# Reordered last batch, mask as a bank term, weight parts turned by DMA, and 16-bit views in a six-layer kernel

## The reference

```python
x = x + cross_attention0(layernorm(x), ctx)   # 16 heads of 32, biases bq bk bv, out: concat @ Wo + bo
x = x + state_space(layernorm(x))
# block feed-forward: 16 blocks of 128, of which each token keeps the 4 most probable
prob = softmax(xf @ router_w.T + router_b); mask = top 4 of 16
h = relu(where(mask, x @ w1_block + b1_block, 0))
x = x + (where(mask, h, 0) @ w2 + b2)
x = x + cross_attention1(...); x = x + self_attention(...)
# quantised feed-forward, H = 512, I = 1536
up   = act_qdq(act_qdq(x) @ dequant(w_up).T)      # act_qdq: scale = max|.| / 32767, round, clip, * scale
gate = act_qdq(act_qdq(x) @ dequant(w_gate).T)
sig  = round(sigmoid(gate) * 65536) clipped to 65535, / 65536
gate = act_qdq(gate * sig); o = act_qdq(gate * up)
x = x + o @ dequant(w_down).T                     # dequant: blocks of 32 columns, 4 bits
```

## Time and profile before

| | us |
|---|---|
| median of 3 runs (lowest, highest) | 1790.96 (1788.42, 1792.11) |
| the profiled execution's own time | 1786.74 |
| span of its trace | 1785.0 |

### The profile page before, as it was taken

How to read it: one execution, slowest core, us unless ns; L and a number is a source line. 1 busy time by engine, 2 the same in 40 slices (tenths; PEclk the granted TensorE clock), 3 DMA queues, 4 the chain that set the end, 5 groups by cost and what they waited for, 6 DMA issues and landing times. The chain is left out here.

```text
span 1785.0 us, 34095 instructions
## 1 busy us (share of the span) xinstructions
PE 1586.5 (89%) x13897; PEld 828.1 (46%) x14008; DVE 1181.6 (66%) x1991; ACT 914.9 (51%) x1259; POOL 800.0 (45%) x406
## 2 busy tenths in 40 slices
PE   5999999999999999987689899899789989699359
PEld 2445555555555555543346464345434444344124
DVE  6688888888888888883455467779522233527881
ACT  1378888787877888773273133311112222228750
POOL 2277887888888888863108514522000000003310
PEclk9999999999999999998799979999899999899779
DMA  3589999999999999997316541234748944000001
GB/s 137 141 150 197 193 189 192 188 191 191 195 189 191 193 195 196 190 165 160 85 53 214 166 195 54 77 123 129 283 167 326 399 165 193 1 1 1 0 1 48
DMA packets 517543, 273.31 MB, mean 153 GB/s; under 512 B 443776, under 2 KB 495488, under 8 KB 514320
## 3 DMA queue, kind: packets, MB, share of 16 engines
q1 hardware_dynamic: 517392, 271.18, 63.3%
HBM read 138.74 MB, written 22.54 MB: 90 GB/s over the span
## 5 line engine op out<-in xcount | busy, mean ns | idle before, releaser
L553 POOL TENSOR_TENSOR x<-x_prob,x 128x1604 bf16<-128x1604 f32 x120 | 388.0, 3233 | 145.0 <-ACT x L708 145.0
L831 DVE TENSOR_REDUCE x_negmax<-x_score 128x1 f32<-128x1604 f32 x128 | 233.5, 1824 | 15.7 <-PE x_score L594 5.9
L690 ACT ACTIVATE x_prob<-x_score,x_negmax 128x1604 f32<-128x1604 f32 x128 | 204.8, 1600 | 43.9 <-DVE x_negmax L831 39.0
L577 PE MATMUL x_ring<-x_ctx_hi,wk_split 128*128 128x400 bf16 (+1 forms) x1024 | 216.2, 333 | 0.3 <-DVE x_kT L767 0.3
L577 PE MATMUL x_ring<-wv_split,x_ctx_hi 128*128 128x512 bf16 (+1 forms) x770 | 200.3, 379 | 9.7 <-issue 7.0
L767 DVE SCALAR_TENSOR_TENSOR x_kT<-x_ring,bk,x_kT 128x400 bf16<-128x400 f32 (+1 forms) x256 | 162.1, 634 | 31.9 <-ACT x_kT L679 23.9
L708 ACT CAST x<-x_prob 128x1604 bf16<-128x1604 f32 x120 | 183.0, 1525 | 0.0
L773 DVE TENSOR_TENSOR x_v<-x_ring,x_v 128x512 bf16<-128x512 f32 (+1 forms) x208 | 143.7, 691 | 52.9 <-ACT x_v L683 50.1
L679 ACT ACTIVATE x_kT<-x_ring,bk 128x400 bf16<-128x400 f32 (+1 forms) x196 | 116.0, 592 | 71.8 <-PE x_ring L577 71.0
L610 PE MATMUL x_pv<-x_pT,x_v 128*64 128x128 bf16 (+1 forms) x3328 | 119.9, 223 | 27.7 <-DVE x_kT L794 17.0
L683 ACT CAST x_v<-x_ring 128x512 bf16<-128x512 f32 (+1 forms) x148 | 86.5, 585 | 98.5 <-PE x_ring L577 98.3
(11 more groups left out here) (336 smaller groups left out, 2576.5 us busy)
## 6 DMA issues: line engine op xcount, KB each, us to landing
y_ctx<-in_ctx SPq DMA_DIRECT2D x16, 1664.0 KB, 10.6
y_ctxT<-in_ctxT SPq DMA_DIRECT2D x16, 1601.0 KB, 13.9
x_stage<-in_ctxT SPq DMA_DIRECT2D x48, 400.0 KB, 4.5
x_q_rows<-q_rows SPq DMA_DIRECT2D x64, 128.0 KB, 3.2
m_xT<-in_L_ffn_w SPq DMA_DIRECT2D x16, 512.0 KB, 4.8
ffn_w_parts<-m_xT SPq DMA_DIRECT2D x32, 256.0 KB, 2.6
x_stage<-in_ctxT SPq DMA_DIRECT2D x16, 401.0 KB, 5.0
f_w<-ffn_w_parts SPq DMA_DIRECT2D x4, 1024.0 KB, 9.8
```

The source lines that it names most:

```text
L553: pool.tensor_tensor(ph[:, g % 2, 1, 0:NKP], prob[:, g % 2, :], ph[:, g % 2, 0, 0:NKP], ALU.subtract).then_inc(pl_done, 1)
L577: last = pe.matmul(out_, lhs, rhs, start=(i == 0), stop=(i == len(steps) - 1))
L690: nc.scalar.activation(prob[:, g % 2, :].rearrange("p (c n) -> p c n", n=QW), scores, ACT.Exp, bias=nmax[:, g % 2:g % 2 + 1], accum_out=rs ...
L831: dve.tensor_reduce(nmax[:, pair % 2:pair % 2 + 1], scores, mybir.AxisListType.XY, ALU.max, negate=True).then_inc(max_done, 1)
```

## The change

Four parts.

1. Cross attention 0, last batch: the output tile comes directly behind the scores instead of last in the slot. bv no longer goes through `catT`; a product of bv with Wo in slot 0 ("bias") is added to bo, which now lies in `stage` and is loaded at g = LAST - 3. x is loaded again in eight DMAs spread over slots 2 to 6. DVE makes the last pair's low part instead of POOL. In slot 2 of that batch ACT finishes its pair before it copies the folded bank. At the kernel's start POOL splits the first context batch before it makes `picks`, `tri` and `low`.
2. Block feed-forward: the mask is turned into 0 or -1e30 and added by the mask product into the hidden bank itself, so that ACT's relu gives the masked value; six banks instead of three; DVE's multiply is gone. Four groups are computed before the first mask product.
3. `Dequant`: PE's transposes are replaced by two DMA transposes of the 16-bit parts on SP; ACT and DVE read the piece from SBUF; 17 pieces lie in the hidden layer and 19 in the second; a slot is loaded again when DVE's low part is done.
4. Quantised feed-forward: half of xhat is made by ACT. Rounded values stay in float32 with the large constant and are read as 16-bit integers with a step of two (`whole`, `fraction`), so the steps that remove the constant go away; all elementwise products are DVE's; maxima over partitions go over a PE transpose and a DVE reduction from bank 0. The gate chain ends one tile earlier, and its peak (n = 2) is turned by PE ahead of the last up group. Behind the up products ACT rounds gate for the first three tiles, then up and gate in turn. The last split begins with half a tile.

```diff
 # batch_plan
+        if b == B - 1:
+            steps.append(("tile", p - 1) if p else ("bias", 0))
         if 2 <= NPAIR * b + p < NPAIR * B + 2:
             steps.append(("pv", NPAIR * b + p - 2))
         if b and p == 2:
             steps.append(("out", b - 1))
-        if b == B - 1 and p:
-            steps.append(("tile", p - 1))
 # cross0_batches, SP
+        X_BEHIND = {2: (0,), 3: (1, 2), 4: (3,), 5: (4, 5), 6: (6, 7)}
+                    for t in X_BEHIND.get(g - LAST, ()):
+                        sp.dma_start(home_x[:, t, :], xv[:, t, :]).then_inc(x_in, 16)
 # PE
+            def bias_row(g):
+                pe.wait_ge(wo_in, 16)
+                pe.wait_ge(bv_in, 16)
+                wait_bank(g)
+                for i in range(4):
+                    last_i = pe.matmul(ring[g % RING][:], bvT[:, i:i + 1].broadcast_to([P, P]), wo[:, i, :],
+                                       start=(i == 0), stop=(i == 3))
+                last_i.then_inc(ring_full, 1)
             def output(t, g):
-                pe.wait_ge(cat_done, 8 * (t + 1))
+                pe.wait_ge(ring_free, OUTS[2 * t + 1] + 1)
 # DVE
+            def low_of_last():
+                u = (PAIRS - 1) % 2
+                dve.wait_ge(ph_done, PAIRS)
+                dve.wait_ge(tl_in[u], 16 * (PAIRS // 2 - 1))
+                ph = ph_of[1]
+                dve.tensor_tensor(ph[:, u, 1, 0:NKP], prob[:, u, :], ph[:, u, 0, 0:NKP],
+                                  ALU.subtract).then_inc(pl_last, 1)
+                    if b == B and p == 0:
+                        low_of_last()
 # block_ffn
+        AHEAD = 4
+        hidden_banks = [banks[n] for n in (3, 4, 5, 7, 2, 6)]
-                if n >= 3:
-                    pe.wait_ge(s_relu, n - 2)
+                if n >= 6:
+                    pe.wait_ge(s_masked, n - 5)
             def masks(n):
-                pe.matmul(banks[6 + n % 2][:], sel[:, blk, :], maskT[:, 512 * c:512 * c + 512],
-                          start=True, stop=True).then_inc(s_mt, 1)
+                pe.matmul(hidden_banks[n % 6][:], sel[:, blk, :], maskT[:, 512 * c:512 * c + 512],
+                          start=False, stop=True).then_inc(s_h, 1)
-                nc.scalar.activation(act_out[:, n % 2, :], banks[3 + n % 3][:], ACT.Relu,
-                                     bias=b1[:, blk:blk + 1]).then_inc(s_relu, 1)
+                    act.wait_ge(s_hlo, n - 1)
+                nc.scalar.activation(masked[:, n % 2, :], hidden_banks[n % 6][:], ACT.Relu,
+                                     bias=b1[:, blk:blk + 1]).then_inc(s_masked, 1)
-                dve.tensor_tensor(masked[:, n % 2, :], act_out[:, n % 2, :], banks[6 + n % 2][:],
-                                  ALU.mult).then_inc(s_masked, 1)
 # Dequant
-    EARLY = 13
-    FIRST = 6
+    EARLY = 17
+    FIRST = 5
     def front_at(self, i):
-        return self.FIRST + 2 * i if i < self.EARLY else 32 + i - self.EARLY
+        if i < self.EARLY:
+            return self.FIRST + 27 * i // self.EARLY
+        return 32 + 20 * (i - self.EARLY) // (self.count - self.EARLY)
     def turn_at(self, i):
+        return self.front_at(i) + 2
+        def turn(i):
+            u = i % self.PARTS
+            if i >= self.PARTS:
+                sp.wait_ge(self.s_out[u], 16 * (i // self.PARTS))
+            for h, done in ((0, self.s_hi), (1, self.s_lo)):
+                sp.wait_ge(done, i + 1)
+                sp.dma_start(self.turned[:, u, h].rearrange("p (o c) -> p o c", o=4), self.parts[:, u, h],
+                             transpose=True).then_inc(self.s_turn[u], 16)
         for i in range(self.count):
+            turn(i)
             if i + self.SLOTS < self.count:
                 load(i + self.SLOTS)
+            if i:
+                store(i - 1)
 # quant_ffn
+        whole = [a[:].rearrange("p m n -> p (m n)").bitcast(I16).rearrange("p (m n s) -> p m n s", m=MF, s=2)[:, :, :, 0]
+                 for a in (up, gate)]
+        FIRST = MF - 1
+        STEPS = [range((MF + 3) * m // FIRST, (MF + 3) * (m + 1) // FIRST) if m < FIRST else () for m in range(MF)]
 # PE
+            def spread(n):
+                pe.wait_ge(s_peak, n + 1)
+                pe.transpose(banks[0][:, P * (n - 1):P * n], peak[:, n, 0:1].broadcast_to([P, P]),
+                             ident[:]).then_inc(s_spread, 1)
+                if n == half:
+                    spread(1)
+                if n == half + 2 * FIRST:
+                    spread(2)
+            spread(3)
+            spread(4)
 # DVE, gate chain of tile i, and later tile m
+                    dve.tensor_scalar(tmp[:, i % NB_T, :], tmp[:, i % NB_T, :], 65535.0 / 65536.0, ROUND / 65536.0,
+                                      ALU.min, ALU.add).then_inc(s_s2, 1)
+                    dve.wait_ge(s_s2, i + 1)
+                    dve.tensor_tensor(gate[:, i, :], fraction[:, i % NB_T, :], whole[1][:, i, :],
+                                      ALU.mult).then_inc(s_gs, 1)
+                dve.tensor_tensor(gate[:, m, :], whole[1][:, m, :], whole[0][:, m, :], ALU.mult).then_inc(s_h2, 1)
+                dve.wait_ge(s_h2, m + 1)
+                out_peak(m)
```

More of the change, by code:

```diff
@@ L728, in _ @@
                             todo.pop(0)(pair)
+                        if e[0] == "out" and b == B - 1:
+                            while todo:
+                                todo.pop(0)(pair)
                         seen += 1
@@ L1220 @@
 NB, BW = 16, 128
+OFF = 1e30
 TOPK = NB // 4
@@ L1517, in _ @@
                 k.tile_stats(dve, x, t, (s_out, t + 1))
-            for i in dq.turns(len(groups) + 3 * NT - 1):
-                dq.low_on_vector(dve, i)
 def cross1(k, ident, x):
@@ L2226, in _ @@
             nc.scalar.activation(norm.small[:, 1, :], norm.small[:, 0, :], ACT.Sqrt).then_inc(norm.s_root, 1)
+            act.wait_ge(s_shift, 1)
+            for t in range(NT // 2, NT):
+                nc.scalar.activation(xhat[:, t, :], x[:, t, :], ACT.Identity, bias=shift[:, t:t + 1],
+                                     scale=norm.rstd[:, t, :]).then_inc(s_hat2, 1)
             act.wait_ge(s_big, 1)
@@ L2241, in rounded @@
                 nc.scalar.activation(dst, src, ACT.Identity, bias=big[:], scale=unit[:, n, 1:2]).then_inc(done, 1)
-            for n in range(half):
-                hidden(n)
             def chain(c):
@@ L2251, in chain, with silu @@
                     i = c - 1
-                    act.wait_ge(s_g2, i + 1)
+                    act.wait_ge(s_g1, i + 1)
                     if i >= NB_T:
                         act.wait_ge(s_gs, i - NB_T + 1)
-                    nc.scalar.activation(tmp[:, i % NB_T, :], gate[:, i, :], ACT.Sigmoid).then_inc(s_sg, 1)
-                if 2 <= c <= MF + 1:
-                    i = c - 2
-                    act.wait_ge(s_sg, i + 1)
-                    nc.scalar.activation(tmp[:, i % NB_T, :], tmp[:, i % NB_T, :], ACT.Identity, bias=big[:],
-                                         scale=65536.0).then_inc(s_sr, 1)
+                    nc.scalar.activation(tmp[:, i % NB_T, :], whole[1][:, i, :], ACT.Sigmoid,
+                                         scale=unit[:, 1, 0:1]).then_inc(s_sg, 1)
+            def silu(m):
+                if m == 0:
+                    act.wait_ge(s_unit, 8)
+                rounded(gate[:, m, :], gate[:, m, :], 2, s_h1)
+            for n in range(half):
+                hidden(n)
             for m in range(MF):
```

414 lines of the change are left out of this document (189 added, 225 removed).

## The result

| | kernel before | kernel after |
|---|---|---|
| runs, median (range), us | 1790.46 (1788.42 to 1792.11) | 1748.99 (1744.12 to 1752.91) |
| profiled execution: time, span, us | 1786.74, 1785.0 | 1748.78, 1747.1 |
| ratio after / before | | 0.977, 95% interval 0.974 to 0.979 |

The account below looks back on a forecast made before the run. TensorE was taken as the busiest engine, waiting or burdened in three stretches. Savings of 19 + 26.5 + 9 = 54.5 us took the profiled 1786.74 to 1732.2; with the median 4.2 higher, 1736.5, range 1723 to 1756.

Parts of the forecast that it names:

- A: First cross attention, mainly its last batch: reordered slots and a shorter tail save 19 us, bounds 8 to 23.
- all x tiles in by 8.5: Tail of the last cross attention batch: x reloaded by 8.5 us after the last scores, in a walk saving 2 us.
- At the start: nothing: Kernel start: picks move behind the low parts, queries' spill slips 6 us; no effect, up to 3 us lost.
- B: Block feed-forward: 14.5 (hidden layer) + 12.3 (second layer) + 2 (end) - 2.3 (piece loads) = 26.5 us saved, bounds 14 to 30.
- relu, cast, low part, relu is 2.5 us and stays under 3.02: Block feed-forward's hidden layer: this cycle of ScalarE and GpSimd takes 2.5 us, under TensorE's 3.02 us a group.
- The last piece comes in tile 6: 2 us: End of the block feed-forward: the last low part and store no longer hold the barrier, saving 2 us.
- C: Quantised feed-forward: 7.7 + 1.6 - 0.35 = 9 us saved, bounds 0 to 17.
- the last layer keeps its time: Quantised feed-forward: its last layer takes as long as before, no saving or loss.
- Rival 2: Cross attention's last batch: DMA binds, slots stay near 7 us, A falls by 11: 1747.5 us; chance 0.09.
- Rivals 3 and 4: Quantised feed-forward's 16-bit products: cheap at 0.7 us, 1728.5, chance 0.08; or slow, at 4.0 us 1803.5, chance 0.03.
- Rival 5: Block feed-forward: TensorE runs no further ahead, costing 3 us at most; with the forecast's own range, chance 0.66.
- Rival 1: Block feed-forward: loads and transposes bound the pieces, second layer 95 us or more: 1750.5 us; chance 0.12.

Follow-up runs that it names:

- both edits: Kernel after, with ScalarE casting each group right behind its relu and VectorE's eight bias adds moved to groups 0 to 7: 1743.5 us, ratio 0.975.
- Q's single edit: Kernel after, ScalarE casting each group right behind its relu; theory Q, a serial ring and its shared queue, expected 1738: 1742.9 us.
- D's single edit: Kernel after, VectorE's eight bias adds in groups 0 to 7 instead of 16 to 23; theory D, VectorE is full, expected 1741: 1743.4 us.
- eight edits: The kernel with seven edits, plus the last 19 pieces of the block feed-forward in 17 steps of the second layer instead of 20: 1728.7 us, ratio 0.967.
- the part alone: Kernel before, with only the change's block feed-forward and weight pieces: 1776.8 us, ratio 0.993.
- seven edits: The kernel with five edits, plus ScalarE rounding one product instead of three before the first up rounding, and piece loads issued ahead of the second transpose: 1721.1 us.
- five edits: Kernel after, with cast behind own relu, bias adds in groups 0 to 7, picks behind normalisation, x one pair sooner, second peak's turn behind last up group: 1729.9 us.

## Why the prediction came out as it did

**A, right (19.6 against 19), by two errors that cancel.** The slots came out 3.5 us better: 37.2 us for seven instead of 38.7 and 2 for transposes, since pv waited for a transpose only once, 0.27 us. That the sum came right was luck. The tail lost 0.5 instead of gaining 2: the step "all x tiles in by 8.5" was wrong, they were in at 11.2. The last two tiles stand on SyncE's queue behind a low part's transpose, and the walk let them be issued with the slot. One pair sooner gave 4.2 us back. "At the start: nothing" was right in sum only; it left out both the 5.4 us gained by taking the picks from beside VectorE and the loss of as much by the later spill.

**B, wrong (11.9 against 26.5).** By its own steps: hidden layer 3.4 instead of 14.5, second layer 9.0 instead of 10.0 (12.3 less 2.3), end -0.5 instead of 2. The time of TensorE's own work was right to 0.1 us. The step that failed is "relu, cast, low part, relu is 2.5 us and stays under 3.02". It holds for a group without a piece. It left out what else stands in the three queues of that ring, 17 pieces in 27 groups: on GpSimd a multiply of 1.43 us with up to 2.04 us of wait for VectorE, on ScalarE the piece's cast. And it priced VectorE's part of a piece at 3.5 us from the earlier trace rows, rows of the second layer, where GpSimd is nearly idle; beside GpSimd a piece takes 4.0 to 5.1, and VectorE is full. Window from its first piece to the last mask product, columns as in the earlier trace rows:

```profile
1055.00:1123.20 68.20, 68.18 (x297) 26.77 (x294) 65.73 (x99) 32.67 (x55) 45.45 (x34) 1.00 0.54 140
```

The row that would have warned was in the trace of before: VectorE's bias adds beside GpSimd's low parts and multiplies in the same ring, 1.07 us on average where the shortest take 0.68.

```profile
L1503 DVE TENSOR_TENSOR x<-x,f_b 128x512 f32<-128x512 f32 x8 | 8.6, 1071 | 0.0
```

Shown: casting sooner and relieving VectorE give 5.6 and 5.4 us of the layer's start, 8.2 together; a shorter multiply gives 7.4 and takes 7.5 us off VectorE's busy time. Of the 11.1 us some 8 are so explained. The 6.1 us of wait that remain with both edits, against the 2.5 predicted, are in the trace the same mechanism: a relu that starts late behind a low part, and a last low part that stands behind a piece's multiply. No run took these away. Neither theory held alone: Q's single edit gave half of what Q said, and D's single edit two thirds. "The last piece comes in tile 6: 2 us" failed in the term for the end: the piece did, but its transposes, landing and store follow at 3.3 us a piece on SyncE's queue, and the stage ended 5.4 us behind VectorE's last statistics. The kernel with eight edits shows that this chain set it.

**Behind B, -1.6.** The prediction named this: "wrong if a stage of unchanged code takes another time". TensorE is idle 10.05 us ahead of the next stage instead of 9.15, and its 32 transposes take 6.23 us instead of 5.37. The same shows in the part alone (10.68, 6.18, and 202.8 us for that stage). The longer idle time doesn't decide it. With eight edits TensorE is idle for only 6.28 us there, and the transposes still take 6.25 (granted clock 0.56 in the first 6 us, against 0.71 in the kernel before). With seven edits it is idle for 8.78, the transposes take 5.08, and the stage is 203.3 us long all the same: that kernel loses its time 62 us into the stage, behind a wait of 4.1 us that the kernel before has too: 3 us later the granted clock is still 0.55, and in the kernel before 1.00. What decides how long the clock stays at half is open.

**C, right (7.9 against 9), step by step.** Stall 4.20 us (4.3 predicted), product 1.23 (1.2), step pair 2.39 (2.40), 38.0 us behind the up products (37 to 38). The last up group lost 1.6 us to the clock instead of 2.2. The 1.1 us are in "the last layer keeps its time": from its first product to the end of the span are 68.3 us, against 67.1.

**The rivals.** Rival 2 (slots of 7 us) fell, at 5.1. Rivals 3 and 4 (16-bit products cheap or slow) fell with 1.23 us; with the rule that the prediction cited from the Trainium skill, VectorE: DVE Perf Modes, section What auto-detection actually checks, the trace agrees. Rival 5 fell: four groups ran ahead of the first masks, and the fifth started 34.9 us into the stage (walked: 34.8). Rival 1 gave 1750.5, which the median meets, but not by its mechanism: second layer 87.9 us and not 95, and only some 3 us of the stage were its loads.

## What to carry to other kernels

When an operation goes into a ring of three engines, walk each engine's queue with everything in it, not the ring's own steps: here every queue of the ring held a step of another chain, and moving one step only chose which queue waited. Take the duration of a VectorE operation between SBUF tiles from a stretch where GpSimd is as busy as it will be. And when a slow engine's setup work moves, count both what it releases where it was and who reads its result.

## What the chip showed beyond that

**One unchanged stage has two lengths.** The state space stage took 135.6 to 136.0 us in eight of thirteen profiles and 140.3 to 141.8 in five, with the same code. They part behind the same wait of TensorE, 47 to 49 us into the stage (1.8 us in all). The 6 us behind it in the kernel after (us, busy us (instructions) PE, PEld, DVE, ACT, POOL; clock, DMA share, GB/s):

```profile
917.00:923.00 6.00, 6.00 (x76) 3.77 (x75) 2.99 (x11) 1.83 (x4) 5.84 (x4) 1.00 0.46 123
```

and in the kernel with five edits:

```profile
909.00:915.00 6.00, 5.67 (x43) 3.45 (x44) 1.91 (x6) 0.92 (x2) 5.84 (x4) 0.50 0.48 123
915.00:925.00 10.00, 9.68 (x107) 6.04 (x103) 4.40 (x14) 2.66 (x5) 7.98 (x5) 0.84 0.72 224
```

TensorE keeps its full clock in the one. In the other it is granted half for 6 us and 0.84 on average in the next 10, about 9 us at half and so 4.6 lost, which is the stage's difference. Up to there its waits in the stage differ by 0.3 us in sum (3.6 and 3.9). What tips it is open. These 4.7 us are as much as several of the edits above are worth, and they may be part of what separates the runs of one kernel, which no run here shows by stage; that is why the edits were read by stage.

**GpSimd's picks made a 128x8 operation of VectorE ten times longer** (1.63 us against 0.17). Each of the three picks takes 2.1 us, so what such a neighbour costs goes by the length of its instruction and not by the size of the operation that waits.
